# Four conditioned residual layers on one core: mixed blocks split from doubled rows, the mask multiplied after mixing, and layer 3's bias rows written into PSUM by ScalarE

## The reference

```python
# layer 0: the two best of 8 experts (256 -> 1024 -> 256, gelu gate) and a shared one
x = x + sum_e w[b,e] * mlp_e(x) + mlp_shared(x)
# layer 1: a matrix of its own for every batch, mixed from 8, masked
w_b = einsum('bg,got->bot', c, weight * mask)
x = x + einsum('bnt,bot->bno', x, w_b) + bias
# layer 2: a base product and 8 low-rank terms of rank 16, weighted by c
x = x + x @ W_base.T + b_base + 2.0 * sum_e c[b,e] * (x @ A_e.T) @ B_e.T
# layer 3: the best of 8 experts (256 -> 512 -> 256, silu gate), with biases
up, gate = x @ wu_e.T + bu_e, x @ wg_e.T + bg_e
x = x + (silu(up) * gate) @ wd_e.T + bd_e
```

## Time and profile before

| what | value |
|---|---|
| time, median of 3 runs | 1377.16 us (1370.75 to 1379.93) |
| the profiled execution | 1381.71 us, its span 1380.1 us |
| mean granted TensorE clock in it | 0.967 of full speed |
| PE, PEld busy | 1278.1 us, 1160.4 us |
| DVE, ACT, POOL busy | 707.0, 414.5, 619.6 us |
| transfers | 122.82 MB, mean 89 GB/s |

### The profile page before, as it was taken

How to read it: one execution, slowest core, us unless ns; L and a number is a source line. 1 busy time by engine, 2 the same in 40 slices (tenths; PEclk the granted TensorE clock), 3 DMA queues, 4 the chain that set the end, 5 groups by cost and what they waited for, 6 DMA issues and landing times.

```text
span 1380.1 us, 29485 instructions
## 1 busy us (share of the span) xinstructions
PE 1278.1 (93%) x8230; PEld 1160.4 (84%) x8231; DVE 707.0 (51%) x1163; ACT 414.5 (30%) x816; POOL 619.6 (45%) x409
## 2 busy tenths in 40 slices
PE   8776897999999999999999999899999985999997
PEld 7676887888888888888888889899898974888886
DVE  6944453544545445454544544767777752333333
ACT  4122332232222222222222222334233321333332
POOL 4900046703425053442544800876656648888000
PEclk9988898999999999999999999999999997999999
DMA  7359993301213022121312210222322213444111
GB/s 199 100 128 263 253 264 90 106 14 44 76 30 89 13 61 61 42 76 30 91 42 76 61 61 15 70 92 92 108 84 83 78 49 99 133 128 132 44 44 39
DMA packets 134578, 122.82 MB, mean 89 GB/s; under 512 B 66033, under 2 KB 116465, under 8 KB 134529
## 3 DMA queue, kind: packets, MB, share of 16 engines
q1 hardware_dynamic: 116880, 59.71, 16.6%
q0 software_dynamic: 17648, 62.48, 14.7%
HBM read 88.07 MB, written 25.69 MB: 82 GB/s over the span
## 4 chain that ended last, share of the span: by engine, by line
PE 70%; POOL 10%; SPq 7%; DVE 5%; issue 5%; DMA 2%; ACT 1%; POOLq 0%; DVEq 0%; ACTq 0%
PE bank L590 12%; PE bank L591 12%; PE bank L592 12%; PE bank L642 5%; PE bank L644 5%; PE bank L643 5%; SPq L285 5%; POOL Wl L395 5%; PE bank L627 4%; POOL Wh L393 4%; PE bank L942 1%; PE bank L686 1%; PE bank L941 1%; PE bank L940 1%; PE bank L687 1%
## 5 line engine op out<-in xcount | busy, mean ns | idle before, releaser
L393 POOL TENSOR_TENSOR Wh<-raw,one 128x1024 fp32r<-128x1024 f32 x111 | 214.6, 1934 | 431.2 <-PE bank L644 286.5
L1434 DVE TENSOR_TENSOR FS<-bank,FS 128x512 f32<-128x512 f32 x200 | 138.0, 690 | 283.6 <-PE bank L592 241.2
L395 POOL TENSOR_TENSOR Wl<-raw,Wh 128x1024 fp32r<-128x1024 f32 x111 | 274.8, 2476 | 8.7
L590 PE MATMUL bank<-Wh,RS 128*128 (+1 forms) x576 | 226.3, 393 | 2.9 <-DVE Wl L1524 2.5
L1021 ACT ACTIVATE FS<-bank 128x512 f32<-128x512 f32 x200 | 119.7, 598 | 355.3 <-PE bank L592 354.8
L591 PE MATMUL bank<-Wl,RS 128*128 (+1 forms) x576 | 225.8, 392 | 0.0
L592 PE MATMUL bank<-Wh,RS 128*128 (+1 forms) x576 | 224.4, 390 | 0.0
L642 PE MATMUL bank<-Wh,RS 128*128 (+1 forms) x576 | 175.3, 304 | 4.9 <-DVE RS L1438 4.9
L644 PE MATMUL bank<-Wh,RS 128*128 (+1 forms) x576 | 163.3, 283 | 0.0
L643 PE MATMUL bank<-Wl,RS 128*128 (+1 forms) x576 | 163.1, 283 | 0.0
L590 PE MATMUL bank<-RS,Wh 128*128 128x256 f32 x448 | 136.2, 304 | 6.1 <-issue 6.1
(11 more groups left out here) (213 smaller groups left out, 2570.0 us busy)
## 6 DMA issues: line engine op xcount, KB each, us to landing
raw<-in_w POOLq DMA_DIRECT2D x83, 512.0 KB, 4.1
mixes<-acc SPq DMA_DIRECT2D x16, 1024.0 KB, 6.0
raw<-mixes POOLq DMA_DIRECT2D x32, 512.0 KB, 4.7
FS<-in_xT SPq DMA_DIRECT2D x200, 64.0 KB, 2.2
FS<-x SPq DMA_DIRECT2D x72, 64.0 KB, 2.1
out_rows<-FS SPq DMA_DIRECT2D x72, 64.0 KB, 2.0
acc<-in_x SPq DMA_DIRECT2D x32, 128.0 KB, 3.4
x<-raw SPq DMA_DIRECT2D x16, 256.0 KB, 2.2
```

The costliest lines, as they stand in the source:

```text
L393: pool.tensor_tensor(hi, raw[:, k, :], ones_like(PIECE), ALU.mult).then_inc(done, 1)
L395: pool.tensor_tensor(lo, raw[:, k, :], hi.bitcast(F32), ALU.subtract).then_inc(done, 1)
L590: pe.matmul(ps, ah, bh, start=(i == 0), stop=False)
L1434: TT(hid[h], up_ps[h][:, :], gl[h], ALU.mult).then_inc(hid_done, 1)
```

## The change

Three parts:

1. Blocks for the mixed matrices. `in_w1` now comes as 8 pieces of 128 rows in which every 32 rows stand twice. POOL loads them, three ahead. ACT copies the half (64 rows) of one block into the stacked tile (`stack(n)`, in the odd mixes of `pair_shared`, the first four in the pass before), POOL writes the residual into the other 64 rows. The SBUF to SBUF copies, the mask loads, the masks' products and the early splits go; `mix_weights(n)` waits for `stack_lo`.
2. The mask is loaded once, as two tiles of 128 by 256 (SP), and multiplied into the mixed matrix in `mix_in` (POOL, in place, 128 by 1024 twice). The high parts of the mixed matrix are then made by ACT (`mixed_hi`), the residuals by POOL, and each half's next load is issued behind its residual. DVE's and ACT's orders in the late stage change with it.
3. Layer 3's biases: SP loads the bias rows of every expert to all 128 partitions of `acc` (8 loads of 655 KB), and ACT copies the right rows into the PSUM bank before the products, which then accumulate on them (`start=False`). Up, gate and down have two banks each; five priming products mark these banks, and one the sixth. `pick`, the bias products, `is3` and its six routing instructions, and POOL's building of `rows3` go.

```diff
 # SP
-            def stack(n):
...
             for g in range(4, EARLY):
                 sp.wait_ge(xl_done, g - 1)
                 load_x(g, g % 2)
                 home_x(g - 2)
-                if g % 2 == 1 and g >= WFIRST + 3:
+                if g % 2 == 1 and g >= WFIRST + 5:
                     for n in range(2 * (g - WFIRST - 5), 2 * (g - WFIRST - 5) + 4):
-                        if n >= 0:
-                            spill(n)
-                        stack(n + 4)
+                        spill(n)
...
             sp.wait_ge(tables_ready, 1)
+            sp.dma_start(mask1[:, :], mask[1]).then_inc(mask_in, 16)
...
+            def load_bias3(turns):
+                for t in turns:
+                    e = sp.value_load(chosen3[0:1, t:t + 1], min_val=0, max_val=E - 1)
+                    sp.dma_start(acc[:, BSLOTS * t:BSLOTS * (t + 1), :].rearrange("p a d -> p (a d)"),
+                                 b3[bass.ds(e, 1)].broadcast_to([P, NBIAS])).then_inc(bias3_in, 16)
+
+            sp.wait_ge(x1_done, NU - 2)
+            load_bias3(range(3))
             store_x3(2 * UL - 2, UE + UL - 2)
+            sp.wait_ge(x1_done, NU)
+            load_bias3(range(3, E))
             store_x3(2 * UL - 1, UE + UL - 1)
 # POOL
-            load(0, w1[0])
-            load_mask(0)
-            load(2, w1[1])
+            for m in range(NRAW):
+                load(m, w1[m])
...
+            for n in range(WPIECES):
+                k = n // 2 % NRAW
+                if n % 2 == 0:
+                    pool.wait_ge(raw_in[k], 16 * (n // 6) + 16)
+                pool.wait_ge(stack_hi, n + 1)
+                here, there = half_rows(n), half_rows(n + 1)
+                at = stacked[n % 4]
+                pool.tensor_tensor(at[there, :], raw[here, k, :], at[here, :].bitcast(F32), ALU.subtract)\
+                    .then_inc(stack_lo, 1)
+                pool.wait_ge(stack_lo, n + 1)
+                if n % 2 == 1 and n // 2 + NRAW < WPIECES // 2:
+                    load(k, w1[n // 2 + NRAW])
...
             def mix_in(n, buffer, after=None):
-                for c in range(DC):
+                for i, c in enumerate((1, 0)):
                     pool.wait_ge(raw_in[c], at_raw[c] + 16 * n + 16)
-                    split(c, MAT + 2 * PIECE * buffer + PIECE * c, mix_split, 4 * n + 2 * c)
...
+                    pool.tensor_tensor(here, here, by_batch, ALU.mult).then_inc(masked, 1)
+                for i, c in enumerate((1, 0)):
+                    at = MAT + 2 * PIECE * buffer + PIECE * c
+                    pool.wait_ge(mix_hi, 2 * n + i + 1)
+                    pool.tensor_tensor(Wl[:, at:at + PIECE], raw[:, c, :], Wh[:, at:at + PIECE].bitcast(F32),
+                                       ALU.subtract).then_inc(mix_split, 1)
...
 # PE
+            pe.wait_ge(hid_done, 2 * S1 + 2 * LATE)
+            for ps in (*up3_ps, *gate3_ps):
+                prime(ps[:, :])
+            prime(out3_ps[0][:, 0:D]).then_inc(primed, 1)
             base(NU - 1)
...
-                    pe.matmul(ps[:, :], pick3[:, p, :], rows3[:, k * I3:(k + 1) * I3], start=False, stop=True)\
-                        .then_inc(done, 1)
...
-                pe.matmul(ps, pick3[:, p, :], rows3[:, 2 * I3:2 * I3 + D], start=True, stop=False)
 # ACT
+            def mixed_hi(n, buffer):
+                for i, c in enumerate((1, 0)):
+                    act.wait_ge(masked, 2 * n + i + 1)
+                    at = MAT + 2 * PIECE * buffer + PIECE * c
+                    act.activation(Wh[:, at:at + PIECE], raw[:, c, :], ACT.Copy).then_inc(mix_hi, 1)
...
                 hidden_hi_late(k, 1)
+                mixed_hi(n + 1, 0)
                 x2_hi(n)
                 cross_over(n + 1, UE - 1 + k)
-                gelu_late(k, 2)
                 if not last:
                     split_unit(k + 1, 1 - xset)
+                gelu_late(k, 2)
...
                 gelu_late(k, 3)
+                hidden_hi_late(k, 3)
+                mixed_hi(n + 2, 1)
                 x2_hi(n + 1)
-                hidden_hi_late(k, 3)
...
+            def bias_in_psum(i, ps, part, slots, done, freed=None):
+                e = act.value_load(turn3[0:1, bass.ds(i, 1)], min_val=0, max_val=E - 1)
+                if freed is not None:
+                    act.wait_ge(freed, i - 1)
+                rows_ = acc[:, bass.ds(BSLOTS * e + part, slots), :].rearrange("p a d -> p (a d)")
+                act.activation(ps[:, 0:slots * D], rows_, ACT.Copy).then_inc(done, 1)
...
-                silu(i, first=first)
+                silu(i, p, first=first)
+                if after2:
+                    up_bias(i + 2, p)
                 if after:
                     hi(t3_done, i + 2, x3h, turn3_ps[:, 0:D], x3h_done, gate3_done, i + 1)
-                    pick(i + 1, 1 - p, first=first)
+                if after2:
+                    gate_bias(i + 2, p)
+                out_bias(i, p, first=first or second)
 # DVE
                 x2_lo(n)
-                hidden_lo_late(k, 1)
                 join(n + 1, UE - 1 + k, late=k - 1)
-                hidden_late(k, 2)
                 if not last:
                     split_unit(k + 1, 1 - xset)
+                hidden_lo_late(k, 1)
+                hidden_late(k, 2)
...
                 x2_lo(n + 1)
+                if not last:
+                    join(n + 2, k + 1)
                 hidden_lo_late(k, 3)
                 if not last:
-                    join(n + 2, k + 1)
                     hidden_late(k + 1, 0)
```

More of the change, by code:

```diff
@@ L322, in store_x3 @@
                              x3out.rearrange("p (t d) -> p t d", t=2)).then_inc(x3_stored, 16)
-            for t in range(3):
-                load_late(t)
+            load_late(0)
+            load_late(1)
+            sp.wait_ge(acc_done, S1)
+            sp.dma_start(maskt[0], mask[0]).then_inc(mask_in, 16)
+            load_late(2)
             store_x3(0, 0)
@@ L396, in split @@
                 pool.wait_ge(done, first + 2)
-            def load_mask(n):
-                for e in range(E):
-                    pool.dma_start(raw[e::E, 1, :], mask[n]).then_inc(mask_in, 16)
             pool.wait_ge(first_in[5], 16)
-            load(0, w1[0])
-            load_mask(0)
-            load(2, w1[1])
+            for m in range(NRAW):
+                load(m, w1[m])
             pool.wait_ge(diag_ready, 1)
@@ L469, in _ @@
                 load(i, w0_piece(first_chosen, i))
-            for k in range(4):
-                pool.wait_ge(stack_in[k], 16 * WPIECES)
             expert(0, 1, first_chosen, expert_at(chosen0, 1, E), stacks=True)
@@ L959, in down3, with step3 @@
                 pe.wait_ge(split3, 6 * e + 6)
-                if not first:
-                    pe.wait_ge(y_done, i)
-                ps = out3_ps[:, 0:D]
-                pe.matmul(ps, pick3[:, p, :], rows3[:, 2 * I3:2 * I3 + D], start=True, stop=False)
+                pe.wait_ge(out_pre, i + 1)
+                ps = out3_ps[p][:, 0:D]
                 for c in range(4):
                     wh, wl = weights(at + c * D, D)
-                    pe.matmul(ps, chunk(h3h, c), wh, start=False, stop=False)
-                    pe.matmul(ps, chunk(h3h, c), wl, start=False, stop=False)
-                    mm = pe.matmul(ps, chunk(h3l, c), wh, start=False, stop=(c == 3))
+                    for h, w in ((h3h, wh), (h3h, wl), (h3l, wh)):
+                        mm = pe.matmul(ps, chunk(h, c), w, start=False, stop=(c == 3 and h is h3l),
+                                       skip_group_check=True)
                 mm.then_inc(down3_done, 1)
-            def step3(i, q, before=True, after=True, after2=True, first=False, second=False):
+            def step3(i, q, before=True, after=True, after2=True, first=False):
                 p = q % 2
@@ L978, in step3 @@
                 if before:
-                    down3(i - 1, 1 - p, e_before, first=second)
+                    down3(i - 1, 1 - p, e_before)
                 turn_h(i, first=first)
@@ L986, in _ @@
             turn_x3(0, 0, first=True)
-            pe.wait_ge(rows_step, 4)
-            up_gate3(0, 0, load_expert3(0), first=True)
+            prime(out3_ps[1][:, 0:D]).then_inc(primed, 1)
+            up_gate3(0, 0, load_expert3(0))
             turn_x3(1, 1)
             step3(0, 0, before=False, first=True)
-            step3(1, 1, second=True)
+            step3(1, 1)
             step3(2, 2)
@@ L1033, in hidden_hi_shared, with stack @@
                 act.activation(hh[h], hid[h], ACT.Copy).then_inc(hh_done, 1)
+            def stack(n):
+                k, here = n // 2 % NRAW, half_rows(n)
+                if n % 2 == 0:
+                    act.wait_ge(raw_in[k], 16 * (n // 6) + 16)
+                if n >= 4:
+                    act.wait_ge(mixed_in[1], 2 * (n - 4) + 2)
+                act.activation(stacked[n % 4][here, :], raw[here, k, :], ACT.Copy).then_inc(stack_hi, 1)
             def mix_out(s):
@@ L1048, in mix @@
```

(10 more changed lines are left out.)

147 lines of the change are left out of this document (58 added, 89 removed).

## The result

The changed kernel takes 1406.15 us (median of 4 runs, 1401.59 to 1409.71) beside 1375.77 us for the kernel before on the same chip: ratio 1.0228, 95% interval 1.0187 to 1.0268. It is 2.3% slower. I had predicted 1348 us with a range of 1328 to 1367; the sign is wrong too.

The account below looks back on a forecast made before the run. Bounds taken: DVE in routing, late spills in mixing, PE in experts, SP's queue in layer 3. Routing -11.5, mixing -11, late stage +3, layer 3 -10.5 and +0.5 sum to -29.5, giving 1348 us, range 1328 to 1367.

Parts of the forecast that it names:

- Routing stage: 27 to 66 us: with POOL's splits and mask products gone, DVE's long instructions shorten and PE's two waits go; -11.5 us.
- its spill leaves SP some 3 us earlier and lands in 6 and not 9.4: Mixing stage, 88 to 206 us: PE's longest pause, 9.5 us, shrinks to about 4.5; the stage gains 11 us.
- nothing was ahead of it: Mixing stage: the reason why PE's pause before the first spill lands, 4 us, was expected to stay.
- Rival A: Mixing stage: the spills set the pace and only the last pause goes; costs 8 to 11 us, 1358; chance 0.15.
- base wait: Late stage: ACT's high parts delay x2_hi, so the base product waits 1.2 us in 14 half units; 16.8 us.
- some 15 of the 16.8 are covered: Late stage: DVE's new order removes nearly all of PE's pauses and clock loss, offsetting the base product's waits; sum +3.
- rival B: Port lock returns: POOL's second subtraction delays DVE's join 2 us in 7 units, residuals stretch mixing; 1365; chance 0.15.
- the join falls in the gap in which POOL issues its load: Late stage: DVE's sum x1 + acc was reckoned to escape POOL's second subtraction, which would otherwise make x1 2 us late.
- First mixed matrix: First late-stage unit: the split passes POOL, ACT and POOL again, making the first layer-1 product 1.7 us later.
- so 0.8 us in 23.6 is idle, the floor is 22.8: Layer 3: SP's four-step cycle bounds the loop at 5.70 us a step; eight cycles give 6.3 us of -10.5.
- my own signs: Layer 3, if right: 5.7 us a step, SP never waiting for the result, PE waiting for gathered x.
- D: Layer 3: ACT's three register loads between copies set the step at some 7.0 us; 1398, slower than before; chance 0.05.
- Its own range, with the bounds of parts 2 and 3: Forecast's own range, 1335 to 1362; bounds: mixing stage gain 0 to 24 us, late stage -8 to +20.

Follow-up runs that it names:

- spills_first: Changed kernel with the first two spills of each mixing-stage pass moved ahead of the x loads in SP's queue: 1384.01 us, ratio 1.0041.
- before_no_bias: Kernel before with layer 3's three bias products per step left out, so its output lacks those biases: 1373.77 us, ratio 0.9952.
- l3_loads_ahead: Changed kernel with PE's layer-3 register loads taken earlier, for three of four steps, ahead of the down products: 1410.14 us, ratio 1.0211.
- gather_and_loads: Changed kernel with layer 3's gather issued ahead of the stores and PE's register loads taken in the step before: 1395.36 us, ratio 1.0106.
- short_residual: Changed kernel with POOL's second residual of every mixed matrix cut from 1024 to 64 columns: 1377.64 us, ratio 1.001.
- all_five: Changed kernel with high parts behind cross_over, spills first, gather first, PE's loads ahead and DVE's split of the next x moved later: 1322.7 us, ratio 0.961.
- hi_behind_cross: Changed kernel with ACT's two high parts of the mixed matrix moved behind x2_hi and cross_over: 1362.37 us, ratio 0.987.

## Why the prediction was wrong, point by point

- **Routing stage: right.** 10.5 us of 11.5. The next stage begins at 71.4 to 73.8 us in the ten profiled kernels with the change and at 82.0 to 91.5 us in the four without it, so the sign is safe, and the size depends on the pair that is compared (8 to 20 us). From 17 to 66 us PE doesn't wait at all, and no instruction on the routing takes over 0.35 us where there were 2.89 and 2.70.
- **Mixing stage: the step that failed is "its spill leaves SP some 3 us earlier and lands in 6 and not 9.4"**, with "nothing was ahead of it" for the first. The pauses that I put at 4, 4.5, 4 and 0 us came out at 7.3, 7.1, 5.8 and 1.9. I counted a spill's delay from its issue; it begins when the block is copied. That "the x loads remain ahead of the spill" I had written down, and counted for one pause only; in the kernel before, too, eight x transfers (from 93.03 us) leave ahead of the first spill (99.62). Block 0 was 10 us old when its spill left, in a queue held by an x load that waits for the split of an earlier group (85.03) and by eight transfers of 0.6 us. Taking the copies out left that as it was; with two spills moved ahead of the x loads the stage lost 24.9 us. Rival A foresaw the pauses' length for a reason (bandwidth) that spills_first excludes.
- **Late stage: the base wait was sized right** (1.2 us predicted, 1.00 measured). **The step that failed is "some 15 of the 16.8 are covered"**, and with it my ground against rival B, that "the join falls in the gap in which POOL issues its load". PE's wait for the join did fall, from 7.6 to 2.2 us, but the waits at the turn of the ranks rose from 9.0 us in 10 pauses to 19.7 in 14, and the stage came out 27.7 us longer in place of 1.3. I had asked of one instruction (the join) whether POOL's second subtraction covers it, found that it falls in the gap, and stopped; the next ones on DVE are covered, the splits by 1.4 us and hidden_lo by 2.2. The rival had the right mechanism, in most half units the wrong instruction, and too low a price: 14 half units were hit and not 7. The Trainium skill ("SBUF — State Buffer", section "SBUF: two separate sides") narrows the lock to VectorE's instructions in a mode of two ports and, against a GpSimd instruction that reads SBUF, to those with two SBUF inputs. The rows agree: L1451, L1469 and L1612 (two SBUF inputs) take up to 3.34 us under POOL's work, while L1619 (one input in PSUM) takes 0.69 us at 1016.15 in the midst of a residual. With that rule I could have listed the candidates.
- **First mixed matrix:** 3.5 us in place of 1.7; mechanism right (ACT and POOL in turn, PE waits 6.43 us at 871.36, where it waited 1.11 before), size too low.
- **Layer 3: the step that failed is "so 0.8 us in 23.6 is idle, the floor is 22.8", taken as the time that the loop would reach.** The floor is real (22.53), but the loop does not reach it by lighter products: the stage without them was 0.4 us shorter in before_no_bias and not 10.5. SP waits for a result whose down product waits for x from SP. From the stores at 1342.02 in the kernel after it is 4.1 us to the gather's second transfer, 2.1 to the first register load, 1.8 to the down product, 2.3 to the end of the sum, 0.9 to the next stores: 11.2 us for two steps, 5.6 a step, as much as SP's own work. The products of up and gate lie beside this. Only the order of SP's two jobs and the price of its transfers moved the stage. By my own signs SP would never wait for the result and PE would wait for gathered x. The second came true, for the most part under the label "issue"; SP still waited 0.7 us and more once a cycle.
- **D** (ACT's register loads): no. PE waits for a bias at most once in a run (1.9 us, in l3_loads_ahead, gather_and_loads and short_residual).
- **The range.** "Its own range, with the bounds of parts 2 and 3" was 1335 to 1362, but these bounds added to 1348 give 1324 to 1376. It would have missed 1406 either way.
- What stays open: what starts the second regime of the late stage in the kernel before (below), and how much of layer 3's first half, in the changed kernel and in before_no_bias, goes to late gathers and how much to the expert's weights.

## What to carry to other kernels

Ask of every transfer in an ordered queue when its data was ready, not when it was issued: three stages here were set by where an item stood in a queue (a spill, a gather, two high parts). The changed kernel is 30 us slower than before; all_five, which hardly does more than put its parts in another order, is 3.9% (54 us) faster. Before crediting a removed product, follow the loop through the queues that carry it: an engine that is busy 93% of a stage can still lie beside the ring that sets it. Where instructions of two engines exclude each other, list every instruction of the one under the other's long one, not the one that came to mind.

## What I had not expected of the hardware

- A pause of PE that is labelled "issue" can be a wait for data: the register loads stand behind a semaphore wait in the queue, the products already queued hide that wait, and only the 1.8 us of loads behind it show.
- Short pauses cost more than their length. In hi_behind_cross PE's idle time fell by 26.3 us and its busy time by 15.5 more, with the granted clock at 0.98 and not 0.94.
- The late stage of the kernel before has two regimes. Its half units (from one turn of x2 to the next) take 15.41 us three times running; the sixth takes 19.89, and from there they alternate between 16.05 and 18.31 to 19.33 us. The first regime is the rate without a wait; hi_behind_cross stays at 15.41 and 17.28 up to its last three. The second is the same exclusion as above: from 968.41 DVE's two splits take 4.39 us under POOL's (970.12), and in the half units behind it the join, 0.68 us by itself, takes 2.38 us under POOL's high part (987.38, 987.07). What brings them together just there stays open.
